# Feed-forward products of a cross-attention kernel: from fp32 matmuls to three fp32r matmuls on high and low parts

## The reference

```
# layer 0
q = layernorm(x) @ Wq / 8;  k, v = split(media @ Wkv)          # 16 heads of 64
out = softmax(mask(q k^T)) v                                  # per head
x = x + tanh(attn_gate) * (out @ Wo)
h = layernorm(x, ln_ff_g, ln_ff_b)
h = gelu(h @ W1) @ W2                                         # W1 256x1024, W2 1024x256
x = x + tanh(ff_gate) * h
# layer 1
mp = media @ W_mem^T
ctx = softmax(x mp^T / 16) mp
gate = sigmoid(concat(x, ctx) @ W_gate + b_gate)
out = rmsnorm(x + gate * ctx) * norm_w
```

## Time and profile before

| what | number |
|---|---|
| median of 3 runs | 872.42 us (872.27 to 2096.33) |
| span of the profiled execution | 870.5 us |
| TensorE busy | 833.8 us, 96% of the span |
| VectorE, ScalarE, GpSimd busy | 587.1, 464.3, 401.1 us |
| GpSimd, sums of a pair | 128x1024 additions of 2.4 us, five a pair |

### The profile page before, as it was taken

One profiled execution on the slowest core, in us unless ns is written; L12 is line 12 of the kernel. 1 busy time (PEld: TensorE's weight loads), 2 busy tenths in 40 slices (PEclk: granted clock), 3 DMA queues, 4 the chain that ended last, 5 costly groups with the idle time before them and its releaser, 6 DMA issues.

```text
span 870.5 us, 18230 instructions
## 1 busy us (share of the span) xinstructions
PE 833.8 (96%) x7777; PEld 699.4 (80%) x7777; DVE 587.1 (67%) x968; ACT 464.3 (53%) x727; POOL 401.1 (46%) x189
## 2 busy tenths in 40 slices
PE   4999999999999999999999999999999999998986
PEld 3788878888888788888888888888888778887775
DVE  6856788867567888675677886756788622126375
ACT  4755655657356566573566665735555441126352
POOL 2445565655625656556256565562566650000002
PEclk9999999999999999999999999999999999999999
DMA  9000001000000010000000000000000700000201
GB/s 285 23 1 2 2 2 39 2 2 2 2 1 2 4 37 1 2 2 2 2 1 2 2 1 2 2 2 2 1 2 4 214 1 1 1 1 1 76 1 48
DMA packets 20559, 16.80 MB, mean 19 GB/s; under 512 B 1008, under 2 KB 19456, under 8 KB 20480
## 3 DMA queue, kind: packets, MB, share of 16 engines
q1 hardware_dynamic: 20192, 15.38, 6.0%
q10 hardware_dynamic: 288, 0.27, 0.1%
HBM read 14.59 MB, written 1.05 MB: 18 GB/s over the span
## 4 chain that ended last, share of the span: by engine, by line
PE 78%; DVE 12%; ACT 5%; POOL 2%; issue 1%; DMA 1%; ACTq 0%; POOLq 0%; DVEq 0%
PE psum L1284 21%; PE psum L1298 17%; PE psum L345 13%; PE psum L1253 6%; PE psum L1209 4%; PE psum L1313 3%; PE psum L1060 3%; PE psum L1074 3%; PE psum L1148 2%; DVE mx L901 2%; DVE k_lo L890 2%; DVE ot L931 1%; PE psum L1304 1%; ACT k_hi L608 1%; POOL acc L450 1%
## 5 line engine op out<-in xcount | busy, mean ns | idle before, releaser
L450 POOL TENSOR_TENSOR acc<-acc,ring 128x1024 f32<-128x1024 f32 x128 | 306.7, 2396 | 18.7 <-POOL acc L445 0.5
L901 DVE TENSOR_REDUCE mx<-psum 128x2 f32<-128x800 f32 (+2 forms) x256 | 245.4, 989 | 86.6 <-PE psum L1253 74.7
L631 ACT ACTIVATE ring<-psum 128x1024 f32<-128x1024 f32 x192 | 197.0, 1027 | 64.5 <-PE psum L1284 58.0
L445 POOL TENSOR_TENSOR acc<-ring 128x1024 f32<-128x1024 f32 x32 | 76.9, 2404 | 274.4 <-ACT ring L631 274.4
L1298 PE MATMUL psum<-ring,v 128*64 128x256 f32 (+1 forms) x1664 | 186.7, 381 | 1.7
L1298 PEld LDWEIGHTS psum<-ring,v 128*64 128x64 f32 (+1 forms) x1664 | 116.6, 137 | 61.1 <-DVE k_lo L890 3.9
L1284 PE MATMUL psum<-nm,maskrow 64*128 64x256 f32 (+1 forms) x832 | 123.9, 294 | 0.6 <-ACT ring L631 0.6
L1284 PE MATMUL psum<-q_lo,k_hi 64*128 64x256 f32 (+1 forms) x832 | 116.9, 278 | 0.0
L1284 PE MATMUL psum<-q_hi,k_hi 64*128 64x256 f32 (+1 forms) x832 | 116.8, 277 | 0.0
L1284 PE MATMUL psum<-q_hi,k_lo 64*128 64x256 f32 (+1 forms) x832 | 116.5, 277 | 0.0
L623 ACT COPY od<-psum 128x512 f32<-128x512 f32 x32 | 18.8, 588 | 167.8 <-PE psum L1304 167.8
(11 more groups left out here) (150 smaller groups left out, 1351.4 us busy)
## 6 DMA issues: line engine op xcount, KB each, us to landing
nat<-in_ctx_dram SPq DMA_DIRECT2D x7, 768.0 KB
w<-in_L_xattn_W_dram SPq DMA_DIRECT2D x2, 1024.0 KB, 8.7
wo<-in_L_xattn_Wo_dram SPq DMA_DIRECT2D x1, 1024.0 KB, 9.7
out_dram<-t_res SPq DMA_DIRECT2D x8, 128.0 KB, 1.7
mask<-in_mask_BxS_bk_dram SPq DMA_DIRECT2D x4, 200.1 KB, 7.1
nat<-in_ctx_dram SPq DMA_DIRECT2D x2, 384.0 KB, 7.3
ring<-in_L_xattn_Wkv_dram SPq DMA_DIRECT2D x2, 384.0 KB, 6.2
wq<-in_L_xattn_Wq_dram SPq DMA_DIRECT2D x1, 768.0 KB, 6.7
```

What stands on the lines that cost most here:

```text
L445: nc.gpsimd.tensor_tensor(acc[:, :, :, :], ring[:, 0, :, :, :], ring[:, 1, :, :, :], ALU.add)\
L450: nc.gpsimd.tensor_tensor(acc[:, :, :, :], acc[:, :, :, :], ring[:, g, :, :, :], ALU.add)\
L631: nc.scalar.activation(ring[:, g, :, :, :], score_set[m % 2].rearrange("p (h i q) -> p h i q", h=2, i=2), ACT.Exp).then_inc(S["p_ready"], 1)
L901: nc.vector.tensor_reduce(mx[:, t, :, c], pair[:, :, 0:min(c1, KEYS) - c0], axis=AX.X, op=ALU.max).then_inc(S["m_max"], 1)
```

## The change

`hidden` and `ff_out` no longer multiply fp32 numbers but three products of parts: weights high x tokens high, weights low x tokens high, weights high x tokens low. The parts are made on the chip:

- GpSimd splits W1 and W2, each in four pieces of 512 columns, a cast and a subtraction per piece, ahead of its sums of pair 6 and of pair 7 of the last batch. It waits for the weight's DMA, for which w1 now goes first in SP's queue, ahead of raw_wg, wm and bgate.
- VectorE splits the transposed tokens (items d.i, `split_tokens`, 512 columns) and the gelu's result (items e.i.half, `split_gelu`, 1,024 columns). `ff_zt` now comes from VectorE, when the parts are there.
- h.0.0 moves from behind R(7) to behind S(7, 6).
- On VectorE `ff_sum(0)` and the first half of `split_gelu(2)` now stand ahead of the copy of `combine_weights`' result (`wctx`); before, that copy came first.
- All tensors of the tail have addresses given by hand, so that the low parts can lie where the fp32 numbers lay and the new tensors find room.

```diff
-               ("R", 7): "w.0 h.0.0", ("S", 7, 6): "h.0.1 g.0.0 g.0.1", ("A", 7): "h.1.0",
-               ("D", 7): "z.2 g.1.0 h.1.1 g.1.1"}
+               ("R", 7): "w.0 d.0 d.1", ("S", 7, 6): "h.0.0 h.0.1 g.0.0 g.0.1", ("A", 7): "h.1.0 e.0.0 e.0.1",
+               ("D", 7): "z.2 g.1.0 h.1.1 g.1.1", ("F", 7): "d.2 e.1.0 e.1.1"}
...
-        w1 = ph("w1", [P, DT, FF])
+        w1, w1_lo = at(0, "w1", [P, DT, FF]), at(0, "w1_lo", [P, DT, FF], F32R)
+        w1_hi = at(8 * KB, "w1_hi", [P, DT, FF], F32R)
...
+            def split_ff_weights(n):
+
+                raw, hi, lo, landed = ((w1, w1_hi, w1_lo, "w1_in"), (w2, w2_hi, w2_lo, "w2_in"))[n]
+                pieces = 4
+                pool.wait_ge(S[landed], 16)
+                for i in range(pieces):
+                    at_once = [t.rearrange("p a n -> p (a n)")[:, 512 * i:512 * (i + 1)] for t in (hi, raw, lo)]
+                    nc.gpsimd.tensor_copy(at_once[0], at_once[1]).then_inc(S["ff_w_hi"], 1)
+                    pool.wait_ge(S["ff_w_hi"], pieces * n + i + 1)
+                    nc.gpsimd.tensor_tensor(at_once[2], at_once[1], at_once[0].bitcast(F32), ALU.subtract)\
+                        .then_inc(S["ff_w_split"], 1)
+
             def sums(b, next_batch):
 
                 for j in range(PAIRS):
+                    if not next_batch and j >= PAIRS - 2:
+                        split_ff_weights(j - PAIRS + 2)
...
+            def split_tokens(i):
+
+                dve.wait_ge(S["ff_zfull"], i + 1)
+                tail_step(nc.vector.tensor_copy(zts_hi[i][:, :, :], zts[i][:, :, :]))
+                nc.vector.tensor_tensor(zts_lo[i][:, :, :], zts[i][:, :, :], zts_hi[i][:, :, :].bitcast(F32),
+                                        ALU.subtract).then_inc(S["ff_zt"], 1)
+
+            def split_gelu(i, half):
+
+                lane, f = i % LANES, slice(4 * half, 4 * half + 4)
+                dve.wait_ge(S["ff_gelu"], 2 * i + half + 1)
+                tail_step(nc.vector.tensor_copy(gts_hi[lane][:, f, :], gts[lane][:, f, :]))
+                nc.vector.tensor_tensor(gts_lo[lane][:, f, :], gts[lane][:, f, :], gts_hi[lane][:, f, :].bitcast(F32),
+                                        ALU.subtract).then_inc(S["ff_gsplit"], 1)
...
             normalised(BATCH - 1)
+            ff_sum(0)
+            split_gelu(2, 0)
             dve.wait_ge(S["wctx_psum"], 1)
             nc.vector.tensor_copy(wctx[:, :], wctx_psum).then_inc(S["wctx_ready"], 1)
-            ff_sum(0)
+            split_gelu(2, 1)
+            split_tokens(3)
             ff_sum(1)
+            split_gelu(3, 0)
             memory_lo(0)
+            split_gelu(3, 1)
             memory_lo(1)
...
-                    for t in range(DT):
-                        last = mm(dst[:, (f % 4) * TOK:(f % 4 + 1) * TOK], w1[:, t, f * P:(f + 1) * P],
-                                  zts[i][:, t, :], start=(t == 0), stop=(t == DT - 1))
+                    c = slice(f * P, (f + 1) * P)
+                    last = split_mm(dst[:, (f % 4) * TOK:(f % 4 + 1) * TOK],
+                                    [(w[:, t, c], z_t[i][:, t, :]) for t in range(DT)
+                                     for w, z_t in ((w1_hi, zts_hi), (w1_lo, zts_hi), (w1_hi, zts_lo))])
...
-                            pe.wait_ge(S["ff_gelu"], 2 * i + f // 4 + 1)
-                        last = mm(ff2_psum[i][:, t * DIM:(t + 1) * DIM], gts[i % LANES][:, f, t * P:(t + 1) * P],
-                                  w2[:, f, :], start=(f == 0), stop=(f == FT - 1))
+                            pe.wait_ge(S["ff_gsplit"], 2 * i + f // 4 + 1)
+                        for n, (g, w) in enumerate(((hi, w2_hi), (hi, w2_lo), (lo, w2_hi))):
+                            last = mm(ff2_psum[i][:, t * DIM:(t + 1) * DIM], g[:, f, q], w[:, f, :],
+                                      start=(f == 0 and n == 0), stop=(f == FT - 1 and n == 2))
```

More of the change, by code:

```diff
@@ L3 @@
 from contextlib import ExitStack
+import math
 F32 = mybir.dt.float32
@@ L178, in sb @@
             return ctx.enter_context(nc.sbuf_tensor(name, shape, dt))
+        starts, used = {}, [0]
         def ph(name, shape, dt=F32):
+            starts[name] = used[0]
+            used[0] += (mybir.dt.size(dt) * math.prod(shape[1:]) + 31) // 32 * 32
             return phase.enter_context(nc.sbuf_tensor(name, shape, dt))
@@ L230, in cross_attention_kernel @@
         phase.close()
-        w1 = ph("w1", [P, DT, FF])
[L235 to L242, removed]
-        nats = [nat0, nat1]
-        def lanes(name, shape, dt=F32):
-            return [ph(f"{name}{lane}", shape, dt) for lane in range(LANES)]
@@ L249, in cross_attention_kernel @@
[L249 to L267, removed]
+        def at(offset, name, shape, dt=F32):
+            with ExitStack() as spot:
+                if offset:
+                    spot.enter_context(nc.sbuf_tensor(f"below_{name}", [P, offset], U8))
+                return spot.enter_context(nc.sbuf_tensor(name, shape, dt))
@@ new lines, in spread @@
+        def spread(offset, name, shape, n, dt=F32):
+            size = (4 * math.prod(shape[1:]) + 31) // 32 * 32
+            return [at(offset + i * size, f"{name}{i}", shape, dt) for i in range(n)]
+        KB = 1024
+        w1, w1_lo = at(0, "w1", [P, DT, FF]), at(0, "w1_lo", [P, DT, FF], F32R)
+        w1_hi = at(8 * KB, "w1_hi", [P, DT, FF], F32R)
+        w2, w2_lo = at(16 * KB, "w2", [P, FT, DIM]), at(16 * KB, "w2_lo", [P, FT, DIM], F32R)
+        w2_hi = at(24 * KB, "w2_hi", [P, FT, DIM], F32R)
@@ new lines, in cross_attention_kernel @@
+        raw_wg = at(32 * KB, "raw_wg", [P, DT, 2 * DIM])
+        wm = at(36 * KB, "wm", [P, DT, MED])
+        bgate = at(37 * KB, "bgate", [P, DIM])
+        normw = at(38 * KB, "normw", [P, DIM])
+        wctx = at(39 * KB, "wctx", [MED, 2 * DIM])
+        nat1 = at(41 * KB, "nat1", [P, KT, MED])
+        nats = [nat0, nat1]
+        DEAD_Z, DEAD_UNREAD, DEAD_V, DEAD_K, DEAD_RING = [starts[t] for t in ("z", "unread", "v", "k_hi", "ring")]
+        zs = spread(DEAD_Z, "t_z", [P, QT, DIM], 2) + [at(DEAD_UNREAD + 4 * KB, "t_z2", [P, QT, DIM])]
@@ new lines, in cross_attention_kernel @@
+        zs.append(at(DEAD_K + 32 * KB, "t_z3", [P, QT, DIM]))
+        ZT_AT = [DEAD_UNREAD, DEAD_UNREAD + 2 * KB, DEAD_V + 10 * KB, DEAD_K + 34 * KB]
+        zts = [at(spot, f"t_zt{i}", [P, DT, TOK]) for i, spot in enumerate(ZT_AT)]
+        zts_lo = [at(spot, f"t_zt_lo{i}", [P, DT, TOK], F32R) for i, spot in enumerate(ZT_AT)]
+        zts_hi = spread(DEAD_V, "t_zt_hi", [P, DT, TOK], 3, F32R) + [at(DEAD_K + 36 * KB, "t_zt_hi3", [P, DT, TOK], F32R)]
+        wg = at(DEAD_V + 6 * KB, "wg", [P, 2 * DT, DIM])
@@ new lines, in cross_attention_kernel @@
+        gts, gts_lo = spread(DEAD_K, "t_gelu", [P, FT, TOK], LANES), spread(DEAD_K, "t_gelu_lo", [P, FT, TOK], LANES, F32R)
+        gts_hi = spread(DEAD_K + 16 * KB, "t_gelu_hi", [P, FT, TOK], LANES, F32R)
+        MT_SIZE = 4 * KPAD + 24
+        mts_hi = spread(DEAD_RING, "t_mt_hi", [MED, KPAD], LANES, F32R)
+        mts_lo = spread(DEAD_RING + LANES * MT_SIZE, "t_mt_lo", [MED, KPAD], LANES, F32R)
+        free = DEAD_RING + 2 * LANES * MT_SIZE
+        gms_hi, gms_lo = spread(free, "t_gm_hi", [MED, TOK], LANES, F32R), spread(free + 2 * KB, "t_gm_lo", [MED, TOK], LANES, F32R)
@@ new lines, in cross_attention_kernel @@
+        cxs, gxs, gate_s, fuseds, squares, ress = (
+            spread(free + 4 * KB * (i + 1), name, [P, QT, DIM], LANES)
+            for i, name in enumerate(("t_cx", "t_gx", "t_gate", "t_fused", "t_square", "t_res")))
+        uts = spread(free + 28 * KB, "t_u", [MED, TOK], LANES)
+        l1top, l1max, l1den, l1rec, l1sum = (
+            spread(free + 30 * KB + 64 * i, name, [P, QT], LANES)
+            for i, name in enumerate(("t_top", "t_max", "t_den", "t_rec", "t_sum")))
+        p1s = spread(0, "t_p1", [P, QT, KPAD], LANES)
@@ L268, in cross_attention_kernel @@
+        pts = spread(DEAD_K, "t_pt", [P, KT, TOK], LANES)
         ctx.enter_context(phase)
@@ L300, in cross_attention_kernel @@
         NAMES = list(PER) + """norms_in norms_psum norms_ready weights_in consts identity kv_hi kv_split
-            gates_ready gate_weights_in wg_psum wg_ready wctx_psum wctx_ready late_weights_in ff_var ff_rstd ff_z ff_turned ff_zt ff_hidden ff_gelu ff_out x2_ready x2t_psum x2t_ready gm_psum gm_hi_ready gm_lo_ready x0_in x_in mask0_in media0_in tail_step""".split()
+            w1_in w2_in ff_w_hi ff_w_split ff_zfull ff_gsplit gates_ready gate_weights_in wg_psum wg_ready wctx_psum wctx_ready late_weights_in ff_var ff_rstd ff_z ff_turned ff_zt ff_hidden ff_gelu ff_out x2_ready x2t_psum x2t_ready gm_psum gm_hi_ready gm_lo_ready x0_in x_in mask0_in media0_in tail_step""".split()
         LANE_NAMES = """media_in media_t_psum media_hi media_lo pad_ready
@@ L387, in _ @@
             upto(sp, "v_full", BATCH - 1, PAIRS // 2 * GROUPS)
+            sp.dma_start(w1[:, :, :], W1.rearrange("(t p) n -> p t n", p=P)).then_inc(S["w1_in"], 16)
```

(11 more changed lines are left out.)

5 lines of the change are left out of this document (4 added, 1 removed).

## The result

The changed kernel takes 874.58 us (median of 9 runs, 873.97 to 875.99), the kernel before 872.51 beside it: a ratio of 1.0026, with a 95% interval of 1.0017 to 1.0035. It is slower by a quarter of a per cent, where 868.8 was forecast. The profiled execution has a span of 872.9 us against 870.5, where the sum gave 866.9: the forecast is 6.0 us short.

What follows compares the result with a forecast made beforehand. From 691.41 to 783 us almost only TensorE bounds the kernel, so its work and waits count fully. Span 870.5 + 3.6 - 8.2 + 1.0 = 866.9; median 1.9 above, 868.8 us; range 864.5 to 872.4.

Steps and rivals of the forecast that it cites:

- the sum: Profiled execution: 870.5 + 3.6 (O later) - 8.2 (O to scores) + 1.0 (change of kind) = 866.9 us; median 868.8.
- Everything before 690 stays as it is: Last batch: nothing before 690 us changes, nor what follows 783; the whole forecast is about these 92 us.
- GpSimd's split: Ahead of the sums of pair 6: w1 lands 678.7, split takes 7.7 us, ends 686.4; sums end 698.9.
- d.0 and d.1: VectorE's token splits ahead of pair 6's folds: waits for GpSimd's sums cost +1.6 us at acc_ready, bounds 0 to +3.
- The clock: D(6) and S(7) begin at 1.2 GHz after 5 us of idle; about 4 us at half speed, costing 1.9 us.
- sufficed at the end: Argument against a free clock: after the last matmul at 864.06, granted clock was 0.50 from 866.5, 2.4 us later.
- D(6) to O: Half-speed clock +1.9, h.0.0 added +2.84, three halves save 2.3, ScalarE's covered wait -0.3; O near 730.5.
- the near tie: VectorE's e.0.0, e.0.1, reciprocals and ot ready O's operand at 729.3 to 730.3, O near 730.5; cost hidden.
- O to the end: Four halves save 2.45, four ff_out 4.9, idle before 750.21 shrinks from 1.13 to some 0.3: -8.2 us.
- the change of kind: First fp32r matmul behind fp32 work starts its successor late; about seven places, nothing to 1.3 us, taken as +1.0.
- the rivals: Clock and port free, 865.2, 0.20; late weights, 0.12; fp32r saves nothing, 878.6, and clock stays low, 874, 0.03 each.
- late weights: Rival: w1 lands late, holding pair 6's sums and D(6); 875.3 us if landing at 685.2; sign D(6) past 705; 0.12.

Runs made afterwards that it cites:

- e1: Changed kernel with GpSimd's split of w1 behind the sums of pair 6 and of w2 behind those of pair 7; 869.13 us, ratio 0.995 to 0.9975.
- e2: Changed kernel with one wait more: GpSimd begins the split of w1 only when VectorE's six t_z are written; 871.31 us, ratio to before 0.9977 to 0.9995.
- e4: Changed kernel with the edits of e1 and e3, and the gelu's splits moved behind what O waits for; 865.15 us, ratio to before 0.9903 to 0.9928.
- e7: e4 with GpSimd beginning each weight split only when VectorE's fold of pair 6, or 7, is done; 863.80 us, ratio to before 0.9889 to 0.9914.
- e6: Changed kernel with w1's four casts left beside t_z, its four subtractions moved behind the sums of pair 6; 871.69 us, ratio to before 0.999 to 1.0012.
- e3: Changed kernel with d.0 and d.1 behind the fold of pair 6; S(7) waits only for what frees its PSUM bank; 870.16 us, ratio 0.9959 to 0.9981.

## Why the prediction was wrong, and where it was right

**What bounds the kernel: the step that failed.** "Everything before 690 stays as it is." That was not looked into. Of GpSimd's split the prediction asked when it would begin, how long it would take and what of GpSimd's own would come later. It did not ask what VectorE does in those 8 us, though the rows of the gap were at hand. The rule of the Trainium skill that it cites (SBUF — State Buffer, section Who interferes with whom) names tensor_scalar beside copy and cast. Applied to every VectorE instruction beside the new GpSimd work, and not to d.0 and d.1 alone, it would have pointed at t_z. This case's trace agrees with it: 1.1 us for each t_z instead of 0.34.

**d.0 and d.1: the size was wrong.** +1.6 was taken for their waits, from 0 to +3. Four instructions that take 2.2 us alone (0.42 and 0.69, twice) took 5.95 in after, 7.7 in e1 and 8.8 in e2: waits of 3.7 to 6.6, so that the upper bound was too low as well. The bound also had each of them hold up the next sum of GpSimd by its own length; the four sums took 9.94 in after and 10.12 in e2, against 9.95 before, so they were hardly held up. The Trainium skill's rule on the casts, which I gave a sentence and not the sum, held: 2.58 us for the first. And the fold itself, priced as alone at 1.38, takes 2.66 beside the split that follows the sums (2.63 in e4, and 1.38 again in e7, where the split waits for it). I had priced only one side of each meeting. The Trainium skill's rule would have given 870.2 by the sum as it stood; what was missing from that is t_z, the longer fold and the waits beyond +3.

**GpSimd's split.** Landing: 673.55 + 4.9 = 678.4 (678.7 forecast). Duration: 9.0 us (678.55 to 687.5) instead of 7.7, as VectorE holds it up in turn; in e2, where it lies beside VectorE's maxima, which read PSUM, it is 7.8. The start of the sums, 686.4 by the sum, is 690.25, because S(6) was late.

**The clock.** It fell behind D(6) after 4.2 us of idle, as forecast; it cost 1.1 us, not 1.9. It had fallen once before, at 686, where no idle was forecast. That 2.4 us "sufficed at the end" was no sure sign: in e6 and e4 idle of 2.4 and 2.6 us left the clock at 1.00.

**D(6) to O: right in the sum, in part by luck.** Forecast 1.9 + 2.84 - 2.3 - 0.3 = +2.1; measured +2.0. But D(6) to h.0.0 came out at +1.0 instead of +1.6, since the clock cost less, and h.0.0 to O at +1.0 instead of +0.5, since the four halves took 11.8 us where the forecast had 11.3; the two misses cancel. VectorE did not hold O in after; in e1 it did, by 0.2 us: the near tie was real.

**O to the end: nearly right.** Forecast -8.2 + 1.0; measured -8.1. A half takes 2.74 to 2.88, an `ff_out` 5.69 to 5.76, as costed. The +1.0 for the change of kind was too much: the first fp32r matmul costs 0.1 us more behind A(7) (730.21 to 730.43) and 0.2 behind O (743.90 to 744.21), but behind O the others of the half are 0.114 apart instead of 0.118, which gives half of that back.

**The sum.** D(6) is 8.5 later instead of 1.5, 7.0 wrong. Of these, 3.8 lie in the end of the sums of pair 6 (702.70 against 698.9), which wait for the late S(6); 2.0 in d.0 and d.1, which end 3.65 behind the sums instead of 1.6; and 1.2 from there to D(6) (2.8 instead of 1.6), since the fold is longer. The parts behind it came out 1.0 better. That makes the 6.0 us. None of the rivals describes it: the time is near that of late weights, and the sign given for them, D(6) past 705, came, but w1 was in time, so the sign does not tell the two apart.

## What to carry to other kernels

That GpSimd is idle in a gap does not make work put there free: list what VectorE does in the gap, and who waits behind it. In these runs GpSimd's casts, subtractions and sums in SBUF lengthened VectorE's casts, tensor_scalars and two-operand instructions (t_z from 0.34 to 1.10 us, a cast of 512 columns from 0.42 to 2.59), VectorE lengthened GpSimd's casts in turn (0.61 to 1.67), and the engine that waits for VectorE's next result pays for it. When such work must be added, let it start behind the fold or maximum that the chain waits for, and put VectorE's new work behind it as well; e7, which does this, takes 10.5 us less than the changed kernel from the fold of pair 5 to the end. Look then at who reads the new work first: in e7 h.0.0 waited 0.8 us for the split.

## What the runs showed of the hardware

- A tensor_scalar of 128x128 into fp32r (`negl`) took 0.226 us at the median of its 32, and 2.32 in e3 and 1.75 in e2, where it met a sum of GpSimd; a reciprocal from SBUF to SBUF kept 0.49 to 0.55 us beside sums and splits alike. Not every instruction of VectorE waits.
- After 2.4 us (e6) and 2.6 us (e4) of idle, TensorE's granted clock stayed at 1.00; after 4.2 (after), 5.2 (after), 5.5 (e1), 6.8 (e6) and 7.0 (e2) it was 0.50 when work began again or soon behind. At the end of the kernel before it was 0.50 already 2.4 us behind the last matmul, so the length of the idle stretch alone did not decide it.
